# A graph layer's first normalization without its mean: centred weights, a sum of squares on ScalarE, and a residual in one VectorE pass

## The reference

```python
# layer 0, per block of 64 rows (k = 64), Wh = h @ W
scores = softmax(blocks * e[..., None]);  out = scores @ Whc        # e = leaky(Whc @ a)
y = leaky(out @ W1 + b1, 0.01); y = leaky(y @ W2 + b2, 0.01); y = y @ W3 + b3
z = y + out
z = (z - mean(z)) / sqrt(var(z) + 1e-5) * ln_g + ln_b
x1 = layernorm(x + z)
# layer 1, per image, 4 heads of 32 features, h = x1 @ W_proj.T
scores = leaky(s_left[i] + s_right[j] + adj[i, j] * we, 0.2), masked where adj <= 1e-5
x2 = layernorm(leaky(x1 + softmax(scores) @ h + bias, 0.5))
```

## Time and profile before

| | |
|---|---|
| time, median of 3 runs | 2146.17 us (2146.14 to 2150.66) |
| the profiled execution: its own time, its span | 2148.98 us, 2147.2 us |
| busy: PE, weight loads | 1844.1 us (86%), 867.0 us (40%) |
| busy: DVE, ACT, POOL | 1892.5 us (88%), 1588.0 us (74%), 1925.4 us (90%) |
| the costliest group, POOL L449 | 512 of 3460 ns |
| mean granted TensorE clock | 0.962 of full speed |

### The profile page before, as it was taken

How to read it: one execution, slowest core, us unless ns; L and a number is a source line. 1 busy time by engine, 2 the same in 40 slices (tenths; PEclk the granted TensorE clock), 3 DMA queues, 4 the chain that set the end, 5 groups by cost and what they waited for, 6 DMA issues and landing times.

```text
span 2147.2 us, 33672 instructions
## 1 busy us (share of the span) xinstructions
PE 1844.1 (86%) x10854; PEld 867.0 (40%) x10854; DVE 1892.5 (88%) x3667; ACT 1588.0 (74%) x3383; POOL 1925.4 (90%) x761
## 2 busy tenths in 40 slices
PE   6589988898898998899888898899988898888886
PEld 4434434444344443444444443344433443333332
DVE  1189998999989999799998999899997999989997
ACT  6677886787868877688776878678786787666664
POOL 2299998999989999799998999899997999999996
PEclk9699999999999999999999999999999999999999
DMA  3223323233233331323323332332323322232220
GB/s 92 67 87 99 93 90 92 91 103 94 74 105 88 89 113 62 110 88 87 102 88 106 84 98 85 92 99 91 99 84 92 91 87 96 79 105 94 86 76 10
DMA packets 138478, 191.63 MB, mean 89 GB/s; under 512 B 22204, under 2 KB 56384, under 8 KB 138304
## 3 DMA queue, kind: packets, MB, share of 16 engines
q1 hardware_dynamic: 138304, 189.49, 29.8%
HBM read 180.82 MB, written 8.65 MB: 88 GB/s over the span
## 4 chain that ended last, share of the span: by engine, by line
PE 26%; POOL 21%; DVE 20%; issue 15%; ACT 13%; DMA 3%; DVEq 1%; SPq 1%; ACTq 0%; POOLq 0%
PE psum L1023 21%; POOL X L449 19%; DVE X L939 14%; PE psum L1174 4%; DVE X L933 3%; ACT E L706 3%; ACT psum L711 3%; DMA RHO<-rho_scratch 2%; ACT x1s L602 1%; DMA rho_scratch<-rho_T 1%; ACT o_sb L602 1%; ACT accU L684 1%; DVEq L857 1%; ACT pen L669 1%; POOL x1s L421 1%
## 5 line engine op out<-in xcount | busy, mean ns | idle before, releaser
L449 POOL TENSOR_TENSOR X<-RHO,E 128x1536 f32<-128x1536 f32 x512 | 1758.1, 3460 | 129.8 <-ACT E L706 84.3
L939 DVE SCALAR_TENSOR_TENSOR X<-psum,s_j,X 128x512 f32<-128x512 f32 x2048 | 1392.7, 743 | 81.5 <-POOL X L449 70.4
L1023 PE MATMUL psum<-X,haug 128*33 128x512 f32 x4096 | 1009.4, 615 | 6.2 <-DVE X L939 3.1
L706 ACT ACTIVATE E<-psum,we_s 128x512 f32<-128x512 f32 x512 | 397.9, 777 | 381.0 <-PE psum L1023 379.7
L1174 PE MATMUL psum<-ident,adj_sb 128*128 128x128 f32 x2048 | 434.5, 293 | 177.8 <-DVE X L939 176.0
L1174 PEld LDWEIGHTS psum<-ident,adj_sb 128*128 128x128 f32 x2048 | 288.8, 141 | 650.2 <-DVE X L939 484.0
L933 DVE TENSOR_TENSOR X<-psum,E 128x512 f32<-128x512 f32 x512 | 346.3, 676 | 57.6 <-issue 34.5
L711 ACT ACTIVATE psum<-psum,we_s 128x512 f32<-128x512 f32 x512 | 381.8, 746 | 0.0
L1023 PEld LDWEIGHTS psum<-X,haug 128*33 128x33 f32 x4096 | 198.8, 112 | 449.6 <-issue 409.5
L1023 PE MATMUL psum<-sgn_ident,pen 128*128 128x128 bf16 x2048 | 377.7, 220 | 0.0
L669 ACT ACTIVATE pen<-adj_sb,pen_bias 128x512 bf16<-128x512 f32 x512 | 369.2, 722 | 0.8
(11 more groups left out here) (177 smaller groups left out, 1322.7 us busy)
## 6 DMA issues: line engine op xcount, KB each, us to landing
adj_sb<-in_adj_dram SPq DMA_DIRECT2D x128, 1024.0 KB, 5.1
RHO<-rho_scratch SPq DMA_DIRECT2D x32, 1024.0 KB, 9.5
out_dram<-o_sb SPq DMA_DIRECT2D x32, 256.0 KB, 2.8
xg<-in_x_dram SPq DMA_DIRECT2D x28, 256.0 KB, 5.8
blk<-in_adj_dram SPq DMA_DIRECT2D x56, 64.0 KB, 5.7
X<-in_x_dram SPq DMA_DIRECT2D x2, 256.0 KB, 3.0
W_sb<-in_L_gnn_W_dram SPq DMA_DIRECT2D x4, 64.0 KB, 1.8
X<-in_adj_dram SPq DMA_DIRECT2D x4, 64.0 KB, 2.8
```

The costliest lines, as they stand in the source:

```text
L449: Q.tensor_tensor(X[m % NX][:, 0:HP, :], RHO[:, g % 2, 0:HP, :], bc(E[m % NE][:], 1, [P, HP, GROUP]), ALU.mult).then_inc(B_pool, 1)
L706: A.activation(E[m % NE][:], TA[m % NT], ACT.Exp, scale=we_s[:, 3:4], bias=we_s[:, 5:6]).then_inc(E_sb, 1)
L939: ins = V.scalar_tensor_tensor(slot[:, h, :], TA[m % NT], s[:, k, h:h + 1], slot[:, h, :], ALU.mult, ALU.max)
L1023: return T.matmul(o, l, r, start=start, stop=stop)
```

## The change

z is made with no mean. W3 and the identity are centred over the output features (`W3c`, `Cm`), so that y2 @ W3c + out @ Cm is z minus its mean; b3 goes into out's copy `oT` (and out of y1 again through `b1p`). ACT squares the bank in place and sums (`chain_ssq`, once z is complete), which gives the variance. PE then makes z times ln_g anew in the same bank from `W3g` and `Cg`, once the squares are taken, and DVE does x1 = bank * rstd + xb in one pass of four 128-wide parts (`residual`), reading the bank. `chain_zc`, `z_stats`, `z_shift`, `z_norm` and POOL's two `residual` operations go. All dates stand in new tables, each step with its own, and the steps of image 1 that are due before tile 0 run before the loop.

Of the dates before: `z_stats` stood at ZS, `z_rstd` at ZS+3, POOL's and DVE's second halves (`residual`, `r_stats`) at ZS+6, `r_norm` at ZS+10; from PREP followed ACT's `make_diag` (58), `make_factors` (60) and `copy_rho` (61), SP's `store_rho` (61) and POOL's four `make_haug` (61 to 64); the epilogue's steps stood at k = 2 and 4 on PE, 4, 6 and 8 on DVE. In the diff below the four entries of a date are those of u = 0 to 3. The first block that follows the tables is ACT's, then POOL's removed and VectorE's new `residual`, then PE's, then DVE's preparation in the prologue.

```diff
-    MID = ((-5, -4, -3, -2, -1, 0), (7, 8, 9, 10, 11, 12), (19, 21, 22, 23, 24, 25), (30, 31, 32, 33, 35, 37))
-    TAIL = ((13, 14, 15), (26, 27, 28), (38, 39, 40), (50, 51, 52))
-    ZS = (3, 15, 28, 41)
-    PREP = 54
+    AT_PE = {"xT": (-24, -18, 0, 18), "wh0": (-23, -17, 2, 18), "wh1": (-22, -16, 5, 19), "ST": (-10, 8, 20, 30),
+          "oT": (-8, 9, 21, 32), "y1": (-7, 10, 22, 33), "y2": (-6, 11, 23, 34), "z0": (-5, 12, 24, 35),
+          "z1": (-5, 13, 25, 36), "g0": (-2, 15, 27, 38), "g1": (-1, 16, 28, 39), "x1T": (9, 25, 41, 48),
+          "h0": (10, 27, 43, 49), "h1": (11, 28, 44, 50)}
+    AT_ACT = {..., "ssq": (-2, 16, 28, 39), "z_rstd": (1, 18, 29, 41), "r_rstd": (5, 21, 35, 44), "r_norm": (8, 24, 38, 46), ...}
+    AT_DVE = {"max": (-17, -12, 10, 24), "rin": (-14, -10, 13, 26), "res": (1, 18, 30, 41), "r_stats": (3, 19, 33, 41)}
+    AT_POOL = {"xb": (-19, -11, 12, 24), "r_shift": (7, 23, 35, 45)}
+    ONCE_PE = {"rmT": 52, "Rb": 53, "rhoT": 56, "hsum": 57}
+    ONCE_ACT = {"diag": 56, "factors": 58, "rho": 59, "hcol": 63}
+    ONCE_DVE = {"rm": 53, "R4": 54, "lam": 56}
+    ONCE_POOL = {"haug": 59}
+    ONCE_SP = {"rho": 58}
+    EPI_PE = {"back0": 1, "back1": 3}
+    EPI_DVE = {"part0": 4, "part1": 5, "stats": 7}
...
             def chain_oT(c):
-                copy(act_T[set_of(c)], mid_bank(c)).then_inc(oT_sb, 1)
+                if c >= NB + 2:
+                    act.wait_ge(zg_ps, prev(c) + 1)
+                A.activation(oT[set_of(c)], mid_bank(c), ACT.Identity, bias=b3_sb[:]).then_inc(oT_sb, 1)
-            def chain_zc(c):
-                copy(x1_of(c)[:].rearrange("p t f -> p (t f)"), mid_bank(c)).then_inc(zc_sb, 1)
+            def chain_ssq(c):
+                act.wait_ge(z_ps, c + 1)
+                for t in range(GT):
+                    ins = A.activation(mid_bank(c)[:, tsl(t)], mid_bank(c)[:, tsl(t)], ACT.Square,
+                                       accum_out=ssq[v][:, t:t + 1])
+                ins.then_inc(ssq_sb, 1)
...
-                link(Q.tensor_tensor(x1_of(c)[:], x1_of(c)[:], bc(g_bc[:], 1, [P, GT, D]), ALU.mult))
-                Q.tensor_tensor(x1_of(c)[:], x1_of(c)[:], xb[s], ALU.add).then_inc(r_sb, 1)
+            def residual(c):
+                dve.wait_ge(zg_ps, c + 1)
+                dve.wait_ge(rstd_z, c + 1)
+                dve.wait_ge(xb_sb, c + 1)
+                for t in range(GT):
+                    ins = V.scalar_tensor_tensor(x1_of(c)[:, t, :], mid_bank(c)[:, tsl(t)], rstd[s][:, t:t + 1],
+                                                 xb[s][:, t, :], ALU.mult, ALU.add)
+                ins.then_inc(r_sb, 1)
...
             def chain_z(c, j):
-                if j == 0:
-                    mm(mid_bank(c), ones_row[:], b3_row[:], stop=False)
                 for t in range(2 * j, 2 * j + 2):
-                    mm(z, act_T[s][:, tsl(t)], W3_sb[:], start=False, stop=False)
-                    ins = mm(z, ST[s][:, t, :], whe[s][:, t, 0:D], start=False, stop=(t == GT - 1))
+                    mm(z, act_T[s][:, tsl(t)], W3c[:], stop=False)
+                    ins = mm(z, oT[s][:, tsl(t)], Cm[:], start=False)
+            def chain_zg(c, j):
+                pe.wait_ge(ssq_sb, c + 1)
+                for t in range(2 * j, 2 * j + 2):
+                    mm(zg, act_T[s][:, tsl(t)], W3g[:], stop=False)
+                    ins = mm(zg, oT[s][:, tsl(t)], Cg[:], start=False)
...
+            prep(V.tensor_reduce(W3m[:, 0:1], W3_sb[:], AX_X, ALU.add))
+            prep(V.tensor_scalar(W3m[:, 1:2], W3m[:, 0:1], -1.0 / D, None, ALU.mult))
+            prep(V.tensor_scalar(W3c[:], W3_sb[:], W3m[:, 1:2], None, ALU.add))
+            prep(V.tensor_tensor(W3g[:], W3c[:], g_bc[:], ALU.mult))
+            prep(V.tensor_scalar(Cm[:], ident[:], -1.0 / D, None, ALU.add))
+            prep(V.tensor_tensor(Cg[:], Cm[:], g_bc[:], ALU.mult))
...
+            for m in range(-BODY // 2, 0):
+                host(m)
```

More of the change, by code:

```diff
@@ L164, in build_program @@
         rin = [sb(f"rin{v}", [P, GT]) for v in range(6)]
+        ssq = [sb(f"ssq{v}", [P, GT]) for v in range(6)]
         st6 = [sb(f"st6{v}", [P, GT, 6]) for v in range(6)]
@@ L384, in _ @@
                     load_adj(g + 1, k // CHUNK)
-                if k == 8 and (g + 1) % NB != 0:
+                if k == EPI_SP["rho"] and (g + 1) % NB != 0:
                     load_rho(g + 1)
-                if k == 15 and g > 0:
+                if k == EPI_SP["store"] and g > 0:
                     store_out(g - 1)
-                for nb in range(m // BODY, m // BODY + 3):
+                for nb in range(max(m // BODY, 1), m // BODY + 3):
                     n = m - BODY * (nb - 1)
@@ L496, in _ @@
             for c in U:
[L497 to L500, removed]
                 r_shift(c)
@@ L828, in _ @@
             make_hcol(0)
-            chain_ST(NB)
-            chain_oT(NB)
+            for m in range(-BODY // 2, 0):
+                host(m)
             for m in range(MT):
@@ L989, in _ @@
             for c in U:
-                z_stats(c)
+                residual(c)
             for c in U:
@@ L1266, in _ @@
                     chain_z(c, j)
+            for c in U:
+                for j in range(2):
+                    chain_zg(c, j)
             for c in (NB, NB + 1):
@@ L1285, in _ @@
                 make_hsum(0, j)
-            chain_ST(NB)
-            chain_oT(NB)
-            chain_y1(NB)
-            chain_y2(NB)
-            chain_z(NB, 0)
+            for m in range(-BODY // 2, 0):
+                host(m)
             pe.wait_ge(back_in, 16 * H)
@@ L1298, in _ @@
                 host(m)
-                if g > 0 and k in (2, 4):
-                    epi_back(g - 1, k // 2 - 1)
+                for r in range(2):
+                    if g > 0 and k == EPI_PE[f"back{r}"]:
+                        epi_back(g - 1, r)
                 values(m)
```

253 lines of the change are left out of this document (128 added, 125 removed).

## The result

The changed kernel takes 2083.35 us (median of 4; 2076.72 to 2084.10) against 2146.76 (median of 4) for the one before: ratio 0.9688 [0.9669, 0.9707], 63.4 us less. Its profiled execution took 2083.02 us, with a span of 2081.1. The forecast was 2072.

A forecast was written before the change was run, and what follows sets the result against it. POOL came first, DVE and PE within 5%; an image was POOL's work plus waits for RHO and E. 2149.0 - 77 (seven images) + 1 (last) + 2 (prologue) = 2075, less 2.8 to the median: 2072 us, range 2036 to 2112.

The forecast's parts named there:

- The image: Each of seven chain-hosting images: 245.4 us against 256.4, from POOL work 228.9 plus waits 13 and 3.5; -77 us in all.
- PE's crowded tiles: Loop tiles with several PE guests (10, 11, 18, 33, 35): 3.5 us an image of POOL waiting for E.
- the walk: DVE's guests added tile by tile, lag over about 1.5 us handed on to POOL: 13 us of waits an image.
- rival B: In the loop, PE's crowded tiles cost 8 us, not 3.5; an image takes 250, total 2107 us; chance 0.19.
- The boundary: Between images: rho's store goes out about 11 us earlier, so POOL's whole RHO wait goes, 6.5 us an image.
- The residual on DVE: In each chain, four scalar_tensor_tensor of 128 columns on DVE take 1.1 us, between bounds 0.86 and 2.1.
- The last image: The image hosting no chains: epilogue guests at 4, 5, 7 add 0.2 us of lag a group, +1 us.
- The prologue: Before the first tile: `r_norm` about 8 us earlier, chain 4's steps 10 to 12 later, preparations 2; sum +2 (-4 to +7).
- A: Rival: whole kernel goes by the forecast mechanism, images of 243 to 248.5 us, total 2055 to 2094; chance 0.50.
- C: Rival: PE stands before each chain's g0 for late squares, 4.5 us a chain; slower, 2198 us; chance 0.10.
- D: Rival: square is not in ACT's loaded table; two loads of 1.283 us a chain, total 2107 us; chance 0.04.
- PE's stand before `make_Rb`: At tile 53, PE waits for ACT's `make_diag` at 56: 1 to 2 us, once an image.

The follow-up runs named there:

- `aft_xb2`: Changed kernel with POOL's addition xb issued twice, first to a scratch tile; 2083.25 us, ratio 0.9696 to the kernel before.
- the four kernels: Kernel before (2146.76 us) and with rho's store at tile 60, not 61 (2114.08); changed kernel (2083.35) and with that store at 61, not 58 (2140.70).
- `aft_ladder_epi`: Changed kernel with PE doing chain 4's prologue steps ahead of `hsum`, `make_hcol` after tile 1, and the epilogue's old dates; 2065.66 us, ratio 0.9638.
- `aft_epi_old`: Changed kernel with the epilogue's dates of the kernel before put back on PE, ACT and DVE; 2077.26 us, ratio 0.9668.
- `aft_store61`: Changed kernel with only SP's store of rho put back from tile 58 to 61; 2140.70 us, ratio 0.9967.
- `aft_ladder`: Changed kernel with PE doing chain 4's prologue steps ahead of `hsum`, and ACT's `make_hcol` after tile 1; 2070.65 us, ratio 0.9653.
- `aft_rstats1`: Changed kernel with the second normalization's statistics taken of one of four parts and used for all; 2050.39 us, ratio 0.9555.

## Why the prediction was near, and which term of it failed

The time was 11 us above the forecast and well inside the range. By its steps:

*The image* (forecast 245.4, measured 245.7) was right in the sum and nearly in the parts. POOL's work 228.9 against 229.7; DVE 235.3 against 235.1; PE 233 against 226.8 busy, too much, and the two rows stand at different mean clocks (0.97 before, 0.99 after); waits for E 16.5 (13 of DVE's lag and 3.5 of PE) against 15.6; RHO 0 against 0. The doubled operations bear the mechanism out: DVE's guests cost one for one, POOL's nothing. The 3.5 left to PE's crowded tiles were not measured by themselves. What the sum leaves out is the granted clock, with which the middle images lie between 245.0 us at 0.99 and 248.5 at 0.98; that the mean met the forecast within 0.3 is in part luck. That the removed POOL work is worth less than its length is shown by `aft_xb2`, where 5 us put back cost nothing.

The waits do not stand behind two clusters only. Added up by tile over six images, POOL stands 3.5 us an image at tiles 3 to 11, 4.6 at 16 to 30, 4.5 at 39 to 48 and 2.8 at 51 to 57; the walk had 3.4, 3.4, 4.5 and 1.6 for the guests some three tiles earlier, and 3.5 more for PE. Its lower bound of DVE's work, 231.5, should be 234.3 (235.8 - 4 x 0.37), and rival B's 2107 should be 2104; the forecast uses neither.

*The boundary* (6.5 an image, in full) was right in the changed kernel only because the rest of the change stood beside it. (The two parts of "about 11 us earlier" add to 12.2. Measured from the moment POOL was free for the tile, 865.75 before and 1094.2 after, the store is 12.4 us earlier.) The forecast took 6.5 + 4.5 as two terms that add; the four kernels give 4.8 or 8.5 for the boundary and 2.2 or 5.9 for the rest, according to which comes first. In the old kernel 6.5 of wait turned into 4.8 of time, with 1.1 of it back as waits for E and 0.6 not accounted for.

*The residual on DVE*: 1.1 taken, 1.04 measured. *The last image*: +1, measured +1.4. The epilogue's new dates, in the walk a part of the 13 an image, cost the kernel 5.0 to 6.1 us (`aft_ladder_epi`, `aft_epi_old`; 0.9 an image in the second), which the forecast had not set apart and which go with the granted clock, not with DVE's lag.

*The prologue* is the term that failed: +2 was forecast (-4 to +7) and +6.9 came. From `r_norm` to the start of `hsum` both kernels take 20.5 us (77.39 to 97.88, 70.90 to 91.36), so it divides into three. `r_norm` comes 6.5 us earlier where 8 was taken; 1.0 of the difference is the preparations, 2.96 us (22.28 to 25.24) for 2. `hsum` takes 6.93 us where it took 4.40: +2.5 where nothing was taken; with the same prologue it takes 4.20 in `aft_store61`, so this part belongs to the execution and not to the change. From its end to the first exponential it is 15.2 us where it was 4.35 (102.28 to 106.63): +10.9, at the middle of the 10 to 12 worked out, of which the sum used the lower end. -6.5 + 2.5 + 10.9 = +6.9. So chain 4's steps were priced rightly at TensorE's lower level; of the 4.9 missed, 2.5 are the clock over `hsum` in this execution, 1.5 the start of `r_norm`, and 0.9 the lower end of 10 to 12. The forecast did not ask whether another order keeps the chain at the higher one, as `aft_ladder` does, for 12.7 us in all with `hsum` out of the way.

The preparations show a lock, too. `W3g` took 1.25 us beside POOL's addition, which ran from 23.21 to 24.47 and ended 0.15 before it; `Cg`, the same form once POOL was idle, took 0.29. `W3c` took 0.55 beside POOL and `Cm`, the same form, 0.23 without. The Trainium skill ("SBUF — State Buffer", section "SBUF: two separate sides") says that VectorE in a two-port mode, or with two SBUF inputs against a GpSimd operation that reads SBUF, and GpSimd exclude each other for a whole instruction; the trace agrees. By the same rule the residual in the loop, which reads the bank, stays free: its four parts kept 0.26 us of spacing beside POOL, as they did in the prologue with POOL idle (58.91 to 63.05).

*Rivals.* A is what came. C (PE standing before g0) is out: 1.3 us in the whole run where it needed 2.8 a chain; the squares took 0.28 us of spacing each, 1.10 a chain. D is out: one load of 1283 ns. PE's stand before `make_Rb` for ACT's diagonal was forecast at 1 to 2 us an image and measured 2.0.

*Open.* Why `aft_rstats1` gains 3.4 an image at the same granted clock for 2.6 removed; why the clock in the loop falls more often in the changed kernel than in `aft_epi_old`; and how PE's lag passes on, at half for one with the clock equal.

## What to carry to other kernels

Where three engines stand within 5% of each other, ask of each term which engine it leaves as the pace: 11.1 us of work taken from POOL were worth 2.2 or 5.9 us an image with all that came with them, and one DMA in a queue behind a load that it need not follow was worth 8.5 or 4.8. Look at the granted clock of each image, too, before you give a difference of 1% to a date. Give a date its price by its place in the queue, not by its engine's load. In a prologue, where nothing covers, put the products on the path ahead of side work, and look at TensorE's granted clock of the stretch that you move them into.

## What was not expected of the hardware

Over the same 85 to 100 us the granted clock was 0.53 with the 32 one-column products of `hsum` ahead of chain 4, and 0.89 with chain 4 ahead of them. The rows tell what PE did before each, and no more. With one and the same prologue `hsum` took 6.93 us in one execution (0.50) and 4.20 in another (0.86), and with one and the same loop an image took 245.3 us at a mean of 0.99 and 247.8 at 0.98. A further operation on POOL of 1.28 us next to DVE's loop cost nothing at all (`aft_xb2`), and the widest new pass on DVE, 128 columns from the bank with two other inputs, took 0.26 us of spacing for 344 ns of shown duration.
